# Cross-attention on one core: V0b moved to the third head group, x loaded tile by tile, the next batch's Q0 and K0 later

## The reference

```python
q = layer_norm(x, ln1_g, ln1_b)
qh, kh, vh = q @ wq + bq, ctx @ wk + bk, ctx @ wv + bv      # 16 heads of 32
scores = einsum('bqhd,bkhd->bhqk', qh, kh) / sqrt(32)       # causal mask
o = einsum('bhqk,bkhd->bqhd', softmax(scores), vh)
x = x + o @ wo + bo
out = x + gelu(layer_norm(x, ln2_g, ln2_b) @ w1 + b1) @ w2 + b2
```

## Time and profile before

| | us |
|---|---|
| median of three runs (2956.33 to 2957.36) | 2957.35 |
| the profiled execution, its own time | 2956.78 |
| its span in the trace | 2955.1 |
| start of batch 7, of batch 8 | 699.12, 792.33 |
| start of groups 1, 2, 3 of batch 7 | 721.25, 748.54, 772.48 |
| step 2.7 of batch 7 | 763.59 |

### The profile page before, as it was taken

One profiled execution on the slowest core, in us unless ns is written; L12 is line 12 of the kernel. 1 busy time (PEld: TensorE's weight loads), 2 busy tenths in 40 slices (PEclk: granted clock), 3 DMA queues, 4 the chain that ended last, 5 costly groups with the idle time before them and its releaser, 6 DMA issues. The chain is left out here.

```text
span 2955.1 us, 65575 instructions
## 1 busy us (share of the span) xinstructions
PE 2786.7 (94%) x22056; PEld 2510.5 (85%) x22056; DVE 2033.4 (69%) x4884; ACT 1654.5 (56%) x4014; POOL 355.2 (12%) x364
## 2 busy tenths in 40 slices
PE   6999999999999999999984999999999899999999
PEld 4777777787777877777764999999999899999999
DVE  4766676667776677666756877877787766665566
ACT  3655666566655666566644565556556544444444
POOL 1211222112221122212210000000000000000000
PEclk9999999999999999999997999999999999999999
DMA  6666666667665676666634344334435343333442
GB/s 139 112 116 108 111 110 121 114 106 110 118 121 99 114 110 122 115 100 121 98 64 150 136 170 184 135 142 185 170 123 219 135 156 142 142 142 122 155 156 93
DMA packets 151738, 383.03 MB, mean 130 GB/s; under 512 B 12160, under 2 KB 16256, under 8 KB 143488
## 3 DMA queue, kind: packets, MB, share of 16 engines
q1 hardware_dynamic: 151680, 382.28, 52.8%
HBM read 172.51 MB, written 109.05 MB: 95 GB/s over the span
## 5 line engine op out<-in xcount | busy, mean ns | idle before, releaser
L711 ACT ACTIVATE sm<-sm,mins 128x128 f32<-128x128 f32 (+3 forms) x1024 | 571.6, 559 | 570.5 <-DVE mins L574 567.9
L574 DVE CUSTOM_DVE_ANT_0 sm<-bank_s,mask 128x128 f32<-128x128 f32 (+3 forms) x1024 | 480.6, 488 | 418.5 <-PE bank_s L425 416.2
L437 PE MATMUL bank_t<-ident,sm 128*128 128x128 f32 x2560 | 418.8, 278 | 73.8 <-DVE pT L520 37.4
L437 PEld LDWEIGHTS bank_t<-ident,sm 128*128 128x128 f32 x2560 | 299.6, 141 | 178.3 <-issue 58.3
L425 PE MATMUL bank_s<-stack 96*128 96x128 f32 (+3 forms) x1024 | 353.0, 386 | 8.4 <-DMA stack<-st_lo 7.9
L520 DVE COPY pT<-bank_t 128x384 f32<-128x384 f32 (+1 forms) x576 | 326.8, 567 | 1.3 <-PE bank_t L437 1.3
L1092 PE MATMUL bank_x<-b_hi,w_hi 128*128 128x256 f32 x1024 | 296.8, 290 | 26.9 <-ACT g L1515 21.6
L1092 PE MATMUL bank_x<-w_hi,a_hi 128*128 128x256 f32 x1024 | 291.2, 284 | 4.0 <-DVE a_lo L1212 4.0
L1093 PE MATMUL bank_x<-b_lo,w_hi 128*128 128x256 f32 x1024 | 291.1, 284 | 0.0
L1094 PE MATMUL bank_x<-b_hi,w_lo 128*128 128x256 f32 x1024 | 291.1, 284 | 0.0
L1094 PE MATMUL bank_x<-w_hi,a_lo 128*128 128x256 f32 x1024 | 290.9, 284 | 0.0
(11 more groups left out here) (178 smaller groups left out, 7389.4 us busy)
## 6 DMA issues: line engine op xcount, KB each, us to landing
stack<-st_hi SPq DMA_DIRECT2D x256, 256.0 KB, 6.1
xt<-in_x SPq DMA_DIRECT2D x32, 1024.0 KB, 5.1
stack<-st_lo SPq DMA_DIRECT2D x128, 256.0 KB, 7.3
xr<-x_scratch SPq DMA_DIRECT2D x32, 1024.0 KB, 5.6
b_scratch<-b_hi SPq DMA_DIRECT2D x16, 1792.0 KB, 10.0
b_scratch<-b_lo SPq DMA_DIRECT2D x16, 1792.0 KB, 13.7
b_hi<-b_scratch SPq DMA_DIRECT2D x16, 1792.0 KB, 7.5
b_lo<-b_scratch SPq DMA_DIRECT2D x16, 1792.0 KB, 11.2
```

Of the source, the lines that this page charges most:

```text
L437: mm = pe.transpose(bank_t[n % 2][:, P * c:P * c + P], sm[:, n % SLOTS_S, P * c:P * c + P], ident[:])
L574: op = V.tensor_tensor_reduce(sm[:, n % SLOTS_S, off:off + w], bank_s[n % BANKS_S][:, off:off + w], mask[:, 512 - w:512], 1.0, 0.0, ALU.ad ...
L711: op = A.activation(row, row, ACT.Exp, bias=mins[:, g % 2, c:c + 1], scale=-1.0, accum_out=sums[:, g % 2, c:c + 1])
```

## The change

The V0b job moves from steps 10 and 11 of group 1 to steps 5 and 6 of group 2; V1b follows in steps 7 to 9 instead of 5 and 6. O1, O2 and O3 are spread over steps 5 to 10 of group 1. X0 and X1 stand in steps 10 and 11 of group 2, X2 and X3 in steps 0 and 1 of group 3, and behind them Q0 (steps 2, 3), R, K0 (5, 6) and V0a (7 to 9). The next x is loaded tile by tile, each tile as soon as its predecessor in the buffer has been stored, with a semaphore for each tile. Its statistics are taken in steps 1.8, 1.11, 2.1 and 2.4, its normalisation in 2.8 to 2.11. GpSimd makes the next context's blocks 0 and 1 before `expand(it, 2)` and blocks 2 and 3 behind it. The high part of O of group 0 is made in step 11 of group 1 instead of step 10.

```diff
     BESIDE = [
         [("B", {0: 4}), ("Q1", {0: 6, 1: 6}), ("K1", {2: 6, 3: 6}), ("R", {5: 4}), ("V1a", {6: 8, 7: 8, 8: 8}), ("O0", {10: 6, 11: 6})],
-        [("Q2", {0: 6, 1: 6}), ("K2", {2: 6, 3: 6}), ("R", {4: 4}), ("O1", {5: 12}), ("O2", {7: 12}), ("O3", {8: 6, 9: 6}), ("V0b", {10: 12, 11: 12})],
-        [("Q3", {0: 6, 1: 6}), ("K3", {2: 6, 3: 6}), ("R", {4: 4}), ("V1b", {5: 12, 6: 12}), ("X0", {7: 4}), ("X1", {8: 4}), ("X2", {9: 4}), ("X3", {10: 4})],
-        [("Q0", {0: 6, 1: 6}), ("K0", {2: 6, 3: 6}), ("R", {4: 4}), ("V0a", {6: 8, 7: 4, 8: 4, 9: 4, 10: 4})],
+        [("Q2", {0: 6, 1: 6}), ("K2", {2: 6, 3: 6}), ("R", {4: 4}), ("O1", {5: 6, 6: 6}), ("O2", {7: 6, 8: 6}), ("O3", {9: 6, 10: 6})],
+        [("Q3", {0: 6, 1: 6}), ("K3", {2: 6, 3: 6}), ("R", {4: 4}), ("V0b", {5: 12, 6: 12}), ("V1b", {7: 8, 8: 8, 9: 8}), ("X0", {10: 4}), ("X1", {11: 4})],
+        [("X2", {0: 4}), ("X3", {1: 4}), ("Q0", {2: 6, 3: 6}), ("R", {4: 4}), ("K0", {5: 6, 6: 6}), ("V0a", {7: 8, 8: 8, 9: 8})],
     ]
-    R_AT, PV1_AT, PV0_AT, O_PROD_AT, O_HIGH_AT, O_HIGH_LATE = 4, 5, 9, 6, 7, 10
-
-    STATS_AT, NORMALISE_AT = (1, 3, 4, 4), (5, 6, 6, 7)
+    R_AT, PV1_AT, PV0_AT, O_PROD_AT, O_HIGH_AT, O_HIGH_LATE = 4, 5, 9, 6, 7, 11
+
+    STATS_AT, NORMALISE_AT = ((1, 8), (1, 11), (2, 1), (2, 4)), ((2, 8), (2, 9), (2, 10), (2, 11))
...
-            sp.dma_start(xt[:], one(x_v, 0)).then_inc(x_in, 16)
+
+            def load_x(m, t):
+                sp.dma_start(xt[:, t, :], one(x_v, m)[:, t, :]).then_inc(x_in[t], 16)
+
+            for t in range(QT):
+                load_x(0, t)
...
                     stacks(it, g)
-                    if not it.first:
-                        for t in ((0,), (1, 2, 3))[g]:
+                    if it.first and g == 0:
+                        sp.wait_ge(dense, pro.done("X3", 0))
+                    for t in ((0,), (1, 2, 3))[g]:
+                        if not it.first:
                             store(it, t)
-                if it.first:
-                    sp.wait_ge(dense, pro.done("X3", 0))
-                else:
-                    sp.wait_ge(stored, b * 64 + 16)
-                if not it.last:
-                    sp.dma_start(xt[:], one(x_v, b + 1)).then_inc(x_in, 16)
+                            sp.wait_ge(stored, b * 64 + 16 * t - 32)
+                        if not it.last:
+                            load_x(b + 1, t)
                 stacks(it, 2)
...
-                    sp.wait_ge(dense, it.done("X3", 2))
+                    sp.wait_ge(dense, it.done("X3", 3))
                 sp.dma_start(xt[:], one(x_v, b)).then_inc(res_in, 16)
...
-                            x, xg = f"X{m}", 0 if it is pro else 2
+                            x, xg = f"X{m}", 0 if it is pro else 2 + m // 2
                             pe.wait_ge(d_free[it.bank(x, xg)], it.bank_read(x, xg))
...
-                if t == 0:
-                    dve.wait_ge(x_in, m * 16 + 16)
+                dve.wait_ge(x_in[t], m * 16 + 16)
                 V.bn_stats(stats[:, t, :], xt[:, t, :]).then_inc(bn_ok, 1)
...
                     pool.wait_ge(dense, it.done("V1b", 2))
-                    for fb in range(KT):
+                    for fb in range(2):
                         context(it.b + 1, fb)
                 expand(it, 2)
+                if not it.last:
+                    for fb in (2, 3):
+                        context(it.b + 1, fb)
                 o_low(it, 2)
```

More of the change, by code:

```diff
@@ L162, in stage_a @@
         raw_in = [sem(f"raw_in{i}") for i in range(4)]
-        x_in, res_in, stored = sem("x_in"), sem("res_in"), sem("stored")
+        x_in = [sem(f"x_in{t}") for t in range(4)]
+        res_in, stored = sem("res_in"), sem("stored")
         c_in = [sem(f"c_in{i}") for i in range(2)]
@@ L450, in pv @@
                     name = f"V{pair}{'ab'[g // 2]}"
-                    at = {"V0a": -1, "V1a": 0, "V0b": 1, "V1b": 2}[name]
+                    at = {"V0a": -1, "V1a": 0, "V0b": 2, "V1b": 2}[name]
                     pe.wait_ge(d_free[it.bank(name, at)], it.bank_read(name, at))
@@ L641, in body @@
                         o_product(it, g - 1)
-                    if not it.last and not it.tail and g == 2:
+                    if not it.last and not it.tail:
                         for t in range(QT):
-                            if k == STATS_AT[t]:
+                            if (g, k) == STATS_AT[t]:
                                 layer_norm_stats(it.b + 1, t)
                         for t in range(QT):
-                            if k == NORMALISE_AT[t]:
+                            if (g, k) == NORMALISE_AT[t]:
                                 normalise(it.b + 1, t)
```

## The result

The changed kernel takes 2993.4 us (median of four runs, 2991.5 to 2995.0), the kernel before 2956.8 beside it: 1.0124 times, 95% interval 1.0113 to 1.0136, or +36.6 us. Forecast were 2984 us and +26, in a range of 2958 to 3000. The profiled execution took 2992.1 us, with a span of 2990.4.

A forecast was written before the change was run, and what follows sets the result against it. The prediction took PE, busy 94% of the span, as the bound, with DVE setting the X stretch. 14 middle batches by (0.7 + 0 + 1.1) = 25.2, plus 0.5 + 2 - 1.3, gave +26.4 and 2984 us; range 2958 to 3000.

The forecast's parts named there:

- X transposes: Steps 2.10 to 3.2: PE waits for DVE's list before Q0, losing 3.9 us where 3.2 were; +0.7 per batch.
- Copies: Batch's first score: it waits for the stack copies behind the later K0, 9.2 us against 8.1 available; +1.1 per batch.
- V tile and O products: Groups 1 to 3: V0b costs the same in group 2, emptied and refilled steps balance; 0 per batch.
- x by tiles: Loads waiting for each tile's store on SP still arrive in time, about 3 us to spare each; 0.
- POOL's order: Context 0 and 1 done before the reciprocals of 3.1, 2 and 3 before K0's later half in 3.6; 0.
- Ends: Outside the middle batches: prologue +0.5 us, batch 0 +2, last batch -1.3.
- (a): Rival: the stack copies stay hidden and only the X term counts; +11 us, 2968; chance 0.15.
- (c): Rival: terms cancel, X even with before and copies hidden; within 6 us of 2957; chance 0.13.
- (b): Rival: new cover works, X stretch loses 2.0 us instead of 3.2, K0's copies hidden; -18 us, 2939; chance 0.12.
- (d): Rival: ACT late to K0 as to Q0, or PE's clock falls in lighter stretches; +40 to +60, near 3005; chance 0.10.

The follow-up runs named there:

- short_xlow: The changed kernel with the low part of each X tile of the later batches taken over 8 of its 128 columns; 2982.5 us.
- short_copies: The changed kernel with the third and sixth of each six stack copies carrying 256 of 512 columns, in all batches but the first; 2983.9 us.
- k0_late: The changed kernel with K0 in steps 3.7 and 3.8 and V0a in 3.8 to 3.10; 3044.0 us, 1.0296 times before.
- k0_early: The changed kernel with K0 in steps 3.4 and 3.5 instead of 3.5 and 3.6; 2992.9 us.
- x_in_g2_pool: x_in_g2 with GpSimd's order as before the change, context blocks 0 to 3 and then expand; 2944.3 us, 0.9959 times before.
- tiles_only: The kernel before with only the load of x by tiles, its waits and the early statistics; 2957.6 us, 1.0003 times before.
- x_in_g2: The changed kernel with Q0, K0, V0a back as before, all X in 2.10 and 2.11, normalisation in 2.6 to 2.9; 2962.2 us, 1.0020 times before.
- x_covered: The changed kernel with X beside V0b and P·V in 2.7 and 2.9, V1b in 2.5 and 2.6, group 3 as before; 2923.2 us, 0.9886 times before.

## Why the prediction was right, point by point

**Direction, range, size.** Slower was forecast and came; +36.6 us against +26.4, since a middle batch without falls takes 95.25 (95.0 forecast) and since the clock fell.

**X transposes, +0.7 forecast, +0.9 measured.** Q0 was put 8.4 us after the score of 2.10 and stands at 8.64; the loss is 8.64 less 4.5 of work, 4.1, for 3.2 before. The 0.2 us that were missed lie in the first item of the list: the low part of X0 starts 1.84 us after the score (784.46), not 1.6, as ScalarE first copies V1b. From there to the last low part the list was put at 6.0 us and takes 6.0. short_xlow shows that DVE's list carries the stretch. Wrong was the picture of the wait: over 1.5 us before Q0 were promised, 0.47 are there. The rest lies before the transposes of 2.11, 3.0 and 3.1 (0.77, 1.15, 0.68): the same list of DVE, seen at its moves.

**Copies, +1.1 forecast, 0.95 to 1.06 measured; the mechanism right, one limit left out.** Steps 3.10 and 3.11 take 3.26 for the 2.2 they were given; short_copies gives 0.95 back. I counted 9.2 us from K0's end to the last landing, and it is 9.1 (the last matmul of K0 starts at 801.53, the landing is at 810.7); k0_late moves with it. What the sum left out is the limit from Q0, which it named only as a bound of nothing: k0_early shows that it is as late within 0.2 us, so that the term could not have been won back from K0's side. That the two coincide is chance.

**V tile and O products, 0.** Right for group 1, 24.4 us forecast and 24.43 found, for 2.5 to 2.9, in which no wait appeared, and by x_in_g2_pool.

**x by tiles, 0.** Right: tiles_only. **POOL's order, 0.** Right where K0 stands in 3.5; x_in_g2 shows that it costs 0.96 us per batch where K0 stands in 3.2.

**Ends.** Batch 0 took 91.94 us for 90.77, +1.2 where +2 was put; the last batch's way from its first to its last score fell from 88.7 to 86.6, -2.1 where -1.3 was put. The prologue (+0.5 put) ended 0.56 earlier, but it ends between 46.2 and 50.0 in the eight experiments, so nothing can be read from it.

**The sum again, of the profiled executions.** 14 by 2.03 = 28.4; falls of the clock in six batches, 5.8 together over the 95.25; batch 0 and prologue +0.6; last batch -2.1; what follows the last score of stage a, stage b, +2.5, which no edit explains (the clock also falls between the stages, at other places in each kernel). That is 35.2, against 35.3 between the spans. So of the 9 us by which the span grew more than forecast, 5.8 are the clock and 3 the two terms; the ends (2.7 less than put) and what follows stage a (2.5) cancel by luck.

**Rivals.** (a) and (c), copies hidden, fell with the wait of 0.98 us. (b), the cover works, fell for this plan; x_covered, where X stands beside V and P·V, shows such a cover at work. (d) is partly true: the clock fell, in six batches of fifteen, and ScalarE was not late to K0 (its first copy is issued 1.1 us after K0's last matmul starts). The falls were priced far too high as a case of its own (+40 to +60); it should have been a term of a few microseconds in the forecast.

Open stays what makes the clock fall in one batch and not in the next of the same plan. The runs show only where: behind the X stretch of group 3 or behind the wait at the first score. Since x_covered differs from the changed kernel in both stretches, its freedom from falls fits, but no run varied PE's activity alone.

## What to carry to other kernels

A piece of work that VectorE must answer at once costs what VectorE's list exceeds TensorE's work beside it; moving it into steps that are light on TensorE makes the loss larger, and the same piece beside matmuls made the kernel faster. Before a producer is moved later, look for the transfers behind it, count them twice, from the first of the queue and from the last producer, and compare the later with the time left: here 0.3 us were left. And in a list in program order, an item that waits long (`expand`, 5.9 us) must not stand ahead of one that is ready.

## What the runs showed of the hardware

Six copies of 256 KB from SBUF to SBUF on SP's queue land about 2.0 us apart whenever they queue, and take about 14 us from the first issue to the last landing, in the kernel before as in k0_early; three that find the queue empty take 8.0. A copy of half the size landed 0.7 us behind its predecessor, a whole one 1.8 (short_copies against the changed kernel).

A normalise of VectorE (from SBUF to SBUF, 128x512) that starts while GpSimd runs an instruction ends 0.28 to 0.34 us after GpSimd's does, in 300 of 300 cases over all runs, and takes up to 1.3 us instead of 0.54; in the changed kernel VectorE's masks and its moves out of `bank_t` took the same time with GpSimd at work as without (the 384-column move 0.55 us either way).

TensorE's clock can fall to 1.2 GHz for 3.4 us inside a kernel that is bound by TensorE: in the changed kernel behind stretches such as the 5.3 us with 3.45 of work, in k0_late behind an idle 3.31 us. In the changed kernel a fall cost 0.4 to 1.1 us in the X stretch and 1.6 at a batch's first score.
